# A graph layer and a mixture of experts on one core: other chunk ends, the first late outputs in other buffers, ten buffers for fetched rows

## The reference, cut to what matters

```python
x = x + gnn(layernorm(x), src, dst, W, b)      # 6250 nodes x 256, 106250 sorted edges
x = x + ffn(layernorm(x))                      # 8 experts, 2 per node, hidden 1024

def gnn(f, src, dst, W, b):
    msg = (f @ W)[src] * norm_src[src][:, None]
    agg = segment_sum(msg, dst)
    return relu(agg * norm_dst[:, None] + b)

def ffn(x):                                    # layernorm once more, gain and bias by expert
    weights, top_idx = top2(softmax(x @ Wr + br))
    y[e] = gelu(xe[e] @ W1[e] + b1[e]) @ W2[e] + b2[e]
    return sum(weights[:, i] * y[top_idx[:, i]] for i in range(2))
```

## Time and profile before

| | us |
|---|---|
| median of 3 runs (1722.94 to 1727.79) | 1725.7 |
| the profiled execution | 1726.35 |
| its span | 1724.9 |
| PE busy in the span | 1211.3 (70%) |
| POOL busy | 1116.2 (65%) |
| DVE busy | 942.0 (55%) |
| ACT busy | 611.9 (35%) |
| HBM traffic over the span | 204 GB/s |

### The profile page before, as it was taken

The page is one execution under the profiler, slowest core; times in us unless marked ns, Lnnn a source line. Parts: engine busy times, 40 slices in busy tenths (PEclk is TensorE's granted clock), DMA queues, the critical chain, the costliest instruction groups (busy, mean ns, idle before and its releaser), DMA issues.

```text
span 1724.9 us, 26632 instructions
## 1 busy us (share of the span) xinstructions
PE 1211.3 (70%) x9098; PEld 988.4 (57%) x9098; DVE 942.0 (55%) x2432; ACT 611.9 (35%) x1218; POOL 1116.2 (65%) x1112
## 2 busy tenths in 40 slices
PE   6944666576196539973997399669739946879991
PEld 5944435364083318851885188568618735668980
DVE  8996455667153525662566257736635655654440
ACT  4953011111050105521542064244315433445660
POOL 5006777777777777777777777777777137653334
PEclk9998556566596659985998599879859877889996
DMA  5048766855374349755974497487559468888761
GB/s 180 1 110 272 229 214 200 277 170 173 132 259 124 109 163 320 237 155 169 314 252 142 155 328 241 150 294 260 151 166 319 138 195 271 284 268 253 250 194 19
DMA packets 147389, 350.99 MB, mean 203 GB/s; under 512 B 25925, under 2 KB 96103, under 8 KB 130869
## 3 DMA queue, kind: packets, MB, share of 16 engines
q1 hardware_dynamic: 86360, 205.79, 35.0%
q0 software_dynamic: 54528, 137.10, 27.0%
q10 hardware_dynamic: 6364, 6.40, 1.2%
HBM read 291.21 MB, written 59.89 MB: 204 GB/s over the span
## 4 chain that ended last, share of the span: by engine, by line
PE 35%; DMA 26%; POOL 19%; issue 9%; DVE 7%; ACT 2%; SPq 0%; POOLq 0%; DVEq 0%; ACTq 0%
DMA gt<-zt,srcI 12%; PE ps L1189 9%; PE ps L1204 9%; POOL gt L786 8%; PE ps L1103 8%; DMA out<-gt,toks 6%; POOL xs L802 5%; DMA S<-ys,cidx 4%; POOL S L818 2%; PE ps L1078 2%; PE ps L1114 2%; PE ps L1141 2%; POOL out L832 2%; DVE ohl L1278 2%; DMA xb<-xs 1%
## 5 line engine op out<-in xcount | busy, mean ns | idle before, releaser
L786 POOL DMA_INDIRECT gt<-zt,srcI x832 | 840.1, 1010 | 259.9 <-issue 174.1
L1103 PE MATMUL ps<-gt,S 128*128 128x257 f16 x1664 | 354.0, 333 | 182.9 <-DMA gt<-zt,srcI 178.0
L1189 PE MATMUL ps<-xe,w1b 128*128 128x256 f16 x2688 | 349.5, 284 | 53.6 <-DVE xe L1591 48.8
L1103 PEld LDWEIGHTS ps<-gt,S 128*128 128x128 f16 x1664 | 201.9, 152 | 292.4 <-DMA gt<-zt,srcI 274.2
L1189 PEld LDWEIGHTS ps<-xe,w1b 128*128 128x128 f16 x2688 | 272.3, 102 | 99.6 <-DVE xe L1591 54.3
L1204 PE MATMUL ps<-w2b,hT 128*128 128x256 f16 x2688 | 318.5, 276 | 13.9 <-DVE gt L1614 12.5
L1050 ACT ACTIVATE h<-ps,cb 128x256 f32<-128x256 f32 x448 | 227.6, 558 | 276.3 <-PE ps L1189 271.7
L1597 DVE SCALAR_TENSOR_TENSOR hT<-h,cb,hT 128x512 f16<-128x512 f32 x224 | 167.6, 749 | 237.3 <-ACT hT L1054 236.6
L1204 PEld LDWEIGHTS ps<-w2b,hT 128*128 128x128 f16 x2688 | 265.9, 99 | 49.4 <-issue 7.8
L1054 ACT ACTIVATE hT<-h,cb 128x512 f16<-128x512 f32 x224 | 161.7, 722 | 7.3
L802 POOL DMA_INDIRECT xs<-xrow,slI x98 | 97.9, 999 | 71.4 <-ACT xrow L1032 41.9
(11 more groups left out here) (248 smaller groups left out, 1207.6 us busy)
## 6 DMA issues: line engine op xcount, KB each, us to landing
w1b<-ws SPq DMA_DIRECT2D x56, 1024.0 KB
w2b<-ws SPq DMA_DIRECT2D x56, 1024.0 KB, 7.4
ws<-w2b SPq DMA_DIRECT2D x16, 1024.0 KB, 5.2
xb<-xs SPq DMA_DIRECT2D x56, 258.0 KB, 7.5
gt<-zt,srcI POOLq DMA_INDIRECT x832, 3.5
ys<-yb SPq DMA_DIRECT2D x36, 256.0 KB, 7.2
w1b<-in_L_ffn_W SPq DMA_DIRECT2D x8, 1024.0 KB, 8.0
hT<-in_L_ffn_W SPq DMA_DIRECT2D x8, 1024.0 KB, 12.4
```

The source lines that it names most:

```text
L786: e.indirect_dma_start(out=gt[:, i % NG, :], out_offset=None, in_=zt, in_offset=bass.IndirectOffsetOnAxis(ap=srcI[:, c, r:r + 1].bitcast(u ...
L1103: inst = e.matmul(PS[r % 2][:, 0:257], S[:, r % NS, :, c], gt[:, i % NG, part * 257:part * 257 + 257], start=(c == 0 and part == 0), stop= ...
L1189: inst = e.matmul(UP[n % 2][:, z * BS:(z + 1) * BS], w[:, l, kk, j * 128:(j + 1) * 128], xe[m % 2][:, k, kk, :], start=(kk == 0 and l == 0 ...
```

## The change

- The chunks end at tiles 36, 41, 45 and 49 where they ended at 37, 43, 47 and 49. By the same formulas the blocks per chunk become 3, 7, 7, 7, 5, 5, 4 and 18; `M0` becomes 34, `TG` 41, and 22 blocks are late.
- The groups of a chunk are split evenly (3, 3, 4 for ten tiles, 3 and 4 for seven, 2 and 3 for five, one of 4 for each of the last two chunks). There are 15 as before.
- The fetched rows have ten buffers. `S` gets a fourth part, in which the constant `irun` lay apart before, and gives four of them; six are rows 4 to 9 of `xrow` and `xrow2`. The fetch of the fifth tile waits for the landing of the scatters of the last chunk but one. The job of the fetches may have nine chains open.
- The outputs of the first three late blocks go to `yb`, the buffers of the stored ones, when the stores before them have landed, and no longer wait for the edges. The next eight go to `gt`.
- In the planner the rule for a new transpose (`nT`, `xT`) asks whether the last but one has been used, and no longer counts.

```diff
-ENDS = [10, 17, 24, 31, 37, 43, 47, 49]
+ENDS = [10, 17, 24, 31, 36, 41, 45, 49]
+PARTS_OF = [-(-(t1 - t0) // STEP) for t0, t1 in CHUNKS]
+GROUPS = [(c, t0 + (t1 - t0) * i // k, t0 + (t1 - t0) * (i + 1) // k)
+          for c, ((t0, t1), k) in enumerate(zip(CHUNKS, PARTS_OF)) for i in range(k)]
-OFF = [6 if c == LAST - 1 else 0 for c in range(len(CHUNKS))]
+OFF = [MT - (t1 - t0) if c == LAST - 1 else 0 for c, (t0, t1) in enumerate(CHUNKS)]
-NC = 3
+NC = 10
+NCS = 4
...
-            if h and m >= M0 and not (at["tile"] == n and m - M0 < NQ + s["given"]):
+            a = m - M0
+            if h and a >= NY and not (at["tile"] == n and (a < NQ + NY or a < NQ + s["given"])):
...
-                if kind in ("nT", "xT") and s["turned"] - s["used"] >= 2:
+                if kind in ("nT", "xT") and len(turns) >= 2 and turns[-2] not in used:
...
-            fetches.append(Job(fetch_stages(), s["now"]))
+            fetches.append(Job(fetch_stages(), s["now"], width=NC - 1))
...
-        irun = sb("irun", [128, 128, CT], f16)
+        S = sb("S", [128, NS + 1, 128, CT], f16)
+        irun = S[:, NS, :, :]
...
+        def fetched_rows(t, i):
+            k = t % NC
+            return cgb[:, k, i, :] if k < NCS else (xrow, xrow2)[i][:, k, 0:256]
+        def late_rows(a):
+            return yb[(M0 + a) % NY][:, :, :] if a < NY else yq[:, (a - NY) % NQ, :, :]
...
+                    if t == NCS:
+                        for z in range(NSC):
+                            e.wait_ge(s_sc[z], sent(LAST - 1, z))
...
                     a = m - M0
-                    if m < M0:
+                    if a < NY:
                         o = yb[m % NY][:, :, :]
                         if m >= NY:
                             e.wait_ge(s_yst[m % NY], 16 * (m // NY))
                     else:
-                        o = yq[:, a % NQ, :, :]
-                        if a == 0:
+                        o = late_rows(a)
+                        if a == NY:
                             e.wait_ge(s_tile, R * CT)
-                        if a >= NQ:
+                        if a >= NY + NQ:
                             e.wait_ge(s_give[a % 2], 32 * ((a - NQ) // 2 + 1))
```

More of the change, by code:

```diff
@@ L25 @@
 NCH = CT * R // TC
-ENDS = [10, 17, 24, 31, 37, 43, 47, 49]
+ENDS = [10, 17, 24, 31, 36, 41, 45, 49]
 STEP = 4
 CHUNKS = list(zip([0] + ENDS, ENDS))
-GROUPS = [(c, a0, min(a0 + STEP, t1)) for c, (t0, t1) in enumerate(CHUNKS) for a0 in range(t0, t1, STEP)]
+PARTS_OF = [-(-(t1 - t0) // STEP) for t0, t1 in CHUNKS]
+GROUPS = [(c, t0 + (t1 - t0) * i // k, t0 + (t1 - t0) * (i + 1) // k)
+          for c, ((t0, t1), k) in enumerate(zip(CHUNKS, PARTS_OF)) for i in range(k)]
 AFTER = [min(R, -(-(a1 * 128 * NE // N + RE) // RE)) for c, a0, a1 in GROUPS]
@@ L83, with __init__ @@
 class Job:
-    def __init__(self, stages, at=0.0, chunk=None):
+    def __init__(self, stages, at=0.0, chunk=None, width=6):
         self.chunk = chunk
+        self.width = width
         self.stages = collections.deque(collections.deque(s) for s in stages)
@@ L92, in heads @@
     def heads(self):
-        while len(self.open) < 6 and self.stages and self.stages[0]:
+        while len(self.open) < self.width and self.stages and self.stages[0]:
             self.open.append(Chain(self.stages[0].popleft(), self.begin))
@@ L162, in plan @@
     clock = {"PE": 0.0, "DVE": 0.0, "ACT": 0.0, "POOL": 0.0}
-    s = {"now": 0.0, "bank": 0.0, "held": {}, "free": {}, "turned": 0, "used": 0, "norms": -1, "nT": 0, "nW": 0, "hh": 0, "xr": 0, "placed": 0, "tabled": 0, "read": -1, "routed": -1, "loaded": 0, "fetched": False, "asked": False, "given": 0}
+    s = {"now": 0.0, "bank": 0.0, "held": {}, "free": {}, "norms": -1, "nT": 0, "nW": 0, "hh": 0, "xr": 0, "placed": 0, "tabled": 0, "read": -1, "routed": -1, "loaded": 0, "fetched": False, "asked": False, "given": 0}
     later, sent = [], {}
+    turns, used = [], set()
     HAND, SLACK = 0.5, 0.5
@@ L357, in step_job @@
                     s["free"][part] = end
-                s["turned"] += kind in ("nT", "xT")
-                s["used"] += kind in ("nW", "lg")
+                if kind in ("nT", "xT"):
+                    turns.append((kind, arg))
+                if kind in ("nW", "lg"):
+                    used.add(("nT" if kind == "nW" else "xT", arg))
                 if kind in ("wb", "wd", "wf", "hh", "lr", "r5"):
@@ L527, in gnn_ffn @@
         gt = sb("gt", [128, NG, RW], f16)
-        S = sb("S", [128, NS, 128, CT], f16)
         xrow = sb("xrow", [128, MT, XW], f32)
@@ L580, in gnn_ffn @@
         yq = gt[:, :, :].rearrange("p g c -> p (g c)").bitcast(f32)[:, 0:NQ * 2 * D].rearrange("p (q s d) -> p q s d", q=NQ, s=2)
-        cgb = S[:, :, :, :].rearrange("p n d c -> p (n d c)").bitcast(f32).rearrange("p (n s d) -> p n s d", n=NC, s=2)
+        def fetched_rows(t, i):
[3 more added lines that the diff above has]
+            return yb[(M0 + a) % NY][:, :, :] if a < NY else yq[:, (a - NY) % NQ, :, :]
+        cgb = S[:, :, :, :].rearrange("p n d c -> p (n d c)").bitcast(f32).rearrange("p (n s d) -> p n s d", n=NCS, s=2)
         raw = [[w1b[i][:, :].bitcast(f32), hT[i][:, :, :, :].rearrange("p a j c -> p (a j c)").bitcast(f32)] for i in range(2)]
@@ L818, in pool @@
                         e.indirect_dma_start(
-                            out=cgb[:, t % NC, i, :], out_offset=None, in_=ys,
+                            out=fetched_rows(t, i), out_offset=None, in_=ys,
                             in_offset=bass.IndirectOffsetOnAxis(ap=cidx[:, i, t:t + 1].bitcast(u32), axis=0)
@@ L833, in pool @@
                             out=out, out_offset=bass.IndirectOffsetOnAxis(ap=toks[:, a, i:i + 1].bitcast(u32), axis=0),
-                            in_=yq[:, a % NQ, i, :], in_offset=None, bounds_check=N - 1,
+                            in_=late_rows(a)[:, i, :], in_offset=None, bounds_check=N - 1,
                             oob_is_err=False, compute_op=ALU.add).then_inc(s_give[a % 2], 16)
@@ L1625, in vector @@
                     e.wait_ge(s_cg[t % NC], 32 * (t // NC + 1))
-                    then(e.scalar_tensor_tensor(out=row(t), in0=cgb[:, t % NC, 0, :], scalar=wts[:, 0, t:t + 1], in1=row(t),
+                    then(e.scalar_tensor_tensor(out=row(t), in0=fetched_rows(t, 0), scalar=wts[:, 0, t:t + 1], in1=row(t),
                                                 op0=ALU.mult, op1=ALU.add))
-                    e.scalar_tensor_tensor(out=row(t), in0=cgb[:, t % NC, 1, :], scalar=wts[:, 1, t:t + 1], in1=row(t),
+                    e.scalar_tensor_tensor(out=row(t), in0=fetched_rows(t, 1), scalar=wts[:, 1, t:t + 1], in1=row(t),
                                            op0=ALU.mult, op1=ALU.add).then_inc(s_comb, 1)
```

## The result

The changed kernel takes 1684.2 us (median of 4 runs, 1670.7 to 1684.5), beside 1726.4 us for the kernel before on the same chip (4 runs, 1722.9 to 1727.8): a ratio of 0.974, 95% interval 0.969 to 0.979. That is 42 us less, where 51 were forecast (1675 against 1725.7); the time lies within the range. The profiled execution took 1684.5 us, with a span of 1683.0 at a mean clock of 0.817.

A forecast was written before the change was run, and what follows sets the result against it. POOL bounds the edges; then block 35's store, fetches and gives one by one set the end. First fetch 1358, last gather 1470, first give 1488, last give 1666, plus 8.8: 1675 us, 8-in-10 range 1648 to 1703.

The forecast's parts named there:

- The edges' end: End of edge gathers: four more scatters cost 5.2 us; last gather 1348.8, last product about 1354, PE's extra wait 0.
- When fetching can start: POOL's first fetch, after the edges' end and 34 stored blocks: 1354 to 1364, taken as 1358, 56 us earlier.
- Rival B: Fetches start late, at 1396, behind block 33's store; first give 1526, time 1700; chance 0.10.
- The fetches: POOL's 82 fetch gathers at 1.25 us plus 8 scatters: 113 us, bound 132 at old pace; first give 1488.
- The last chunk: Rows PE waits for after the edges: ready at 1408, last scatter issued 1417, first `up` of block 38 at 1429.
- Rivals C and D: C: first `up` 35 us later, 1694 to 1700, chance 0.09. D: adds delay last chunk's routing, 1734, chance 0.07.
- PE's end: PE's late blocks: 1429 + 186 + 24 + 8 for fetch traffic gives last `y` at 1647, 40 us earlier.
- The gives: POOL's 21 intervals between gives from 1488: 16 loaded at 9.25 us (148), five at 6.01 (30); last starts 1666.
- The tail: From the last give's start to the end of the span: 8.8 us, as before.
- The sum: Whole time 1675 us: first give 75 us earlier, the gives take back 25, leaving 50.
- Rival A: PE ends the kernel: late gives cheap, interval near 7.8 us, last `y` 1647, time 1659; chance 0.14.

The follow-up runs named there:

- the early fetch: Changed kernel with `xrow` buffers first, so the first six tiles' fetches skip the last edge product's wait; 1674.9 us, ratio 0.972; on slower chips 1.004 and 1.002.

## Why the prediction was right, step by step

- *The edges' end: right for the product.* The last product is over at 1353.5 for 1354. The last gather is at 1344.49 for 1348.8; the spread between profiles is larger than the 5.2 us of this term, so one profile can't confirm it. The wait of PE for scattered rows that I let stand at 0 is not in this part: the transposes at 1351.33 wait for nothing. PE does stand for 10.00 us, but for an edge gather that lies behind chunk 6's eight scatters (1329.05 to 1338.13) in POOL's own stream, so POOL loses nothing by it:

```profile
1342.25 0.65 PE L1124 MATMUL ps<-gt,S 128*128 128x257 f16 x2 [10.00 <-DMA gt<-zt,srcI]
```

- *When fetching can start: right.* 1354.37, in the 1354 to 1364. The last edge product releases it, as the kernel with the early fetch shows, where the fetch follows at once when that wait is gone. The last stored block's `y` is at 1331.8, and its store is not waited for. Rival B, at 1396, falls.
- *The fetches: right.* 1.32 us a gather for 1.25, last one at 1471.87 for 1470. With the new ends and three buffers it is 1.71, and the phase takes 149 us, more than my bound of 132: the old pace was no bound for an early fetch. That the first give is at 1486.63 for 1488 is in part luck: the first fetch is 3.6 us early, from there to the last gather it is 117.5 us for 112, and the gap to the first give is 3.2 us shorter than in the sum.
- *The last chunk: right.* First scatter 1409.21 for 1408, first `up` of block 38 4 us late:

```profile
1430.08 0.93 PE L1194 MATMUL ps<-ident,xb 128*128 128x128 f32 x4 [3.58 <-DMA xb<-xs]
1433.36 2.93 PE L1210 MATMUL ps<-xe,w1b 128*128 128x256 f16 x13 [2.35 <-DVE xe L1612]
```

  Against the 22.58 us at 1436.88 in the earlier trace rows, no such wait is left. Rivals C and D fall: with ten buffers DVE's adds cost the last chunk nothing that shows, and DVE waits 21.1 us for 66.9.
- *PE's end: right.* Last `y` 1645.9 for 1647. In its place the first `up` is 4 us later and from there to the last `y` it is 212.5 us for 218, so of the 8 us for the fetches' traffic some 2.5 were spent. The DMA engines were full from 1437 to 1480 (share 1.01, 352 GB/s) and PE busy for 33.0 of 43 us; the cost stayed inside PE's slack.
- *The gives: the mis-sized term.* "They are 9.25 us while weights are loaded ... 16 intervals, 148 us." There were 15 in 148.16 us (1486.63 to 1634.79), 9.88 each, and the next six took 36.8 us (6.14 each) for 5 at 6.01: 185.0 for my 178. Twelve of the 15 are 9.0 to 11.8 us long, three 6.2 to 8.4; in the profile of the early fetch the mean is 10.08. That the loads set the price is shown. In like places a loaded give is no dearer than before, though; the 9.25 was a mean over other places. Count the intervals from the last give back: the 9th to the 18th take 96.6 us in the kernel before (1570.00 to 1666.61) and 96.5 in the changed one (1518.62 to 1615.08), 9.7 us each, and 96.0 to 97.6 in the six other profiles of this chip speed with full loads and all gives. The twelve of before hold besides these ten the first, 6.92 us, in which hardly any weights were on their way (SP issues no weight tile between 1556.56 and 1569.08), and the last, 7.46. In the changed kernel there are three in front of the ten, 10.2 to 11.4 us, all beside loads, and two behind, 10.7 and 9.0. What makes one loaded interval dearer than the next stays open: where the gives start at 1520 (the ends alone) and 1538 (ten buffers, old ends), the intervals in front of the ten take 6.6 to 8.7 us beside 158 to 261 GB/s. The rows of the kernel before, its gives and its traffic in and behind the first interval:

```profile
1570.00 1.55 POOL L832 DMA_INDIRECT out<-gt,toks  x1 [3.41 <-DMA out<-gt,toks]
...
1666.61 1.55 POOL L832 DMA_INDIRECT out<-gt,toks  x1 [7.19 <-DMA out<-gt,toks]
```

```profile
1563.00:1570.00 7.00, 7.00 (x67) 6.33 (x65) 2.66 (x5) 4.89 (x10) 3.21 (x3) 1.00 0.53 93
1570.00:1674.00 104.00, 104.00 (x956) 93.61 (x954) 49.63 (x97) 68.88 (x125) 36.09 (x22) 1.00 0.77 244
```

  and the changed kernel, over its 15 intervals:

```profile
1486.00:1635.00 149.00, 149.00 (x1368) 134.13 (x1366) 70.81 (x137) 97.92 (x176) 50.20 (x31) 1.00 0.77 244
```

- *The tail: mis-sized too.* From the last give's second scatter to the end of the span it is 9.5 us for 6.9 before, 8.1 in the kernel with the old ends and ten buffers, 9.2 to 9.5 in those with the new ends, and 11.5 with half of the gives. No instruction stands in it in the trace; what it is, stays open.
- *The sum.* Start 1.4 us early, intervals 7.0 late, tail 2.6 late: 8.2 of the 8.2 us by which the span of 1683.0 misses 1674.8. Rival A (PE ends it) falls: PE is out 26 us before the last give, and making its gives cheap or few is worth 30 us.

## What to carry to other kernels

Where a phase of one engine begins late and runs slowly, an early start and a faster pace are two changes, and each is worth having alone. They can also need one another: with three buffers the early fetches ran slower than the late ones (1.71 us a gather for 1.48), with six or ten at 1.32; four and five were not tried. A chain of transfers in which each waits for the landing of the one before takes its price from other traffic: what it costs beside weight loads (9.7 us) and without (6.1) must both be read, each from intervals that lie wholly in or out of the loads, and moving it under the loads gives back part of the gain, here 32 of 76 us, with two gives more. And a gain measured on one chip may not be there on another whose time differs.

## What the runs showed of the hardware

- Two indirect scatters that add into `out` and wait for the two before take 5.4 us at the least (1666.19 to 1671.62): two issues of 1.55, 0.30 between, 2.0 of waiting. Beside full weight loads (244 GB/s from 1486 to 1635) it is 9.9 in the mean; with an eighth of the loads (88 GB/s from 1480 to 1600) 6.9.
- Two of the chips run these kernels 12 to 16% longer, in the edges above all, at the same duration of each POOL gather (0.95 us) and the same pace of PE at the granted clock of 1.00 (120 us busy of 120 on the usual chip from 1480, 135 of 135 there from 1745), and there a change that is worth 2.6% elsewhere is worth nothing (the changed kernel 1.003 on one; the version with the early fetch 1.004 and 1.002).
